# Two slot sums of a graph attention stream gathered in one PSUM bank before they are added

## The chip, the cores and the metric

The kernel runs on one core of one Trainium2 chip. The metric is the device time of one execution in microseconds (us). A NeuronCore has a matrix engine (TensorE, PE in the profile), a vector engine (VectorE, DVE), a scalar engine (ScalarE, ACT), GpSimd (POOL) and SyncE (SP); matmuls write to PSUM, a memory of eight banks of 512 fp32 words a partition, and DVE and ACT read it.

## The reference

Four graph attention layers run over one graph of 3125 nodes and 53125 edges (25000 pairs in both directions and 3125 loops; layers 0, 1 and 3 add another loop for each node, 56250 edges). Each layer is `x = x + layer(relu(layernorm(x)))` on 256 features. What the edge streams compute is this, here of layer 3, which has two such convolutions (4 heads of 64 channels and 8 heads of 32):

```python
h = (x @ W).reshape(n_nodes, heads, out_ch)
e = leaky_relu(alpha_s[src] + alpha_d[dst], 0.2)
m = segment_max(e, dst)
ex = exp(e - m[dst])
denom = segment_sum(ex, dst)
a = ex / (denom[dst] + 1e-16)
out = segment_sum(h[src] * a[:, :, None], dst)
```

Layers 0 and 1 have one convolution of 4 and of 8 heads over the same edges. Layer 2 has 4 heads, no added loops, edge weights, and sums over the source node instead of the destination.

## The kernel before

A first part sorts the edges twice, by destination (`by_dst`) and by source (`by_src`). A sorted edge list is cut in slots of 128 edges. All edges of a slot belong to one tile of 128 nodes (25 tiles; the last slot of a tile is filled up), so `by_dst` has 464 slots and `by_src` 448. `next_places` finds from a histogram how many slots each tile has, where they start, and which tile a slot belongs to; the tiles of four slots are packed into one integer of `tiles4` (lines 435 to 439). The layers follow one after the other. In each, `gat_layer` makes a table `feats` in DRAM with a row for each node (features, a one for each head, scores), and then `stream_edges` goes once over all slots.

In `stream_edges` the engines work so:

- GpSimd gathers the 128 rows of a slot from `feats` by an indirect DMA (line 1173), four slots a group, into a ring `rows` of 96 slots (48 in layer 3, which has NC = 2 convolutions and so rows twice as wide). A ring place is used again when `slot_sums` says that PE is through with it.
- For a chunk of CS slots (32 in layers 0 and 2, 16 in layers 1 and 3) a chain of four steps makes the probabilities: `score`, `largest`, `carries`, `shift` on DVE, each followed by a small PE piece (`turn_scores`, `turn_ends`, `turn_carry`, `turn_back`). The steps for chunk c+1 stand between the groups of chunk c. Where they stand says the tuple AT: in layers 1 and 3 `score` stands ahead of the chunk's first group of four slots, the others behind groups 0, 1 and 2. PE's `pick_own` fetches the node's own scores with one small matmul a slot (line 1235), in layers 1 and 3 eight of them behind groups 1 and 2.
- The gathered rows are multiplied by the probabilities: in layer 3 ACT does the first convolution slot by slot (line 1330, `messages_too`), DVE the second for four slots in one instruction (`scale`, line 1477, `messages`). With one convolution, DVE takes slots 0 and 2 of four, ACT slots 1 and 3.
- DVE makes a one-hot matrix `oh` of the destinations (`rows_onehot`, line 1459), in halves of two slots.
- PE multiplies one-hot by rows, one slot at a time, into a PSUM buffer of BANKS = 4 // NC, so four in layers 0 to 2 and two in layer 3 (`sums`, line 1281): 260 or 272 columns, or twice 264 in layer 3. Before it, PE waits until DVE has added the slot BANKS earlier (`added`).
- DVE adds the buffer to the accumulator `acc` of the slot's tile (`add`, line 1487), one instruction a slot; in layer 3 it reads both convolutions' banks at once, 528 columns. The tile number comes from `four_tiles` (line 80): a register load and arithmetic on the engine's sequencer.

Every engine's order is written out by hand and unrolled. On DVE a group of four slots is, in this order:

```python
ids = four_tiles(dve, g, gg, T)
if i == 0 and c > 0:
    rescale(c, ids[0])
add(gg, 0, ids)
scale(gg + 1)
add(gg, 1, ids)
rows_onehot(gg + 2, 0, 2)
add(gg, 2, ids)
rows_onehot(gg + 2, 2, 4)
add(gg, 3, ids)
chain(c + 1, i)
```

`rescale` (line 1451) multiplies the open tile's accumulator at a chunk's start by the factor by which the running maximum changed.

## Time and profile before

| | us |
|---|---|
| median of 3 runs | 4905.24 (4902.48 to 4909.39) |
| the profiled execution, its own time | 4901.73 |
| its span, first to last instruction | 4899.9 |
| busy in the span: PE, DVE, ACT, POOL | 3153.6, 3423.1, 2251.0, 2881.1 |
| edge stream of layer 0 (1526 to 2149) | 623 |
| edge stream of layer 1 (2290 to 2909) | 619 |
| edge stream of layer 2 (3049 to 3661) | 612 |
| edge stream of layer 3 (3870 to 4797) | 927 |

The busy times are sums over stages with different limits, so they name no single bound; what a stage waits for is read inside its window. The chain that ended last covers only the last few microseconds here and was not used.
### The profile page before, as it was taken

To read this page: it belongs to the slowest core of one execution; us is meant where nothing else is said; L and a number is where in the kernel's file an instruction comes from. 1 tells how busy PE (TensorE), PEld (TensorE's weight loads), DVE (VectorE), ACT (ScalarE), POOL (GpSimd) and SP (SyncE) were. 2 spreads that over 40 slices of the span, in tenths; PEclk is the share of its full clock that TensorE was granted. 3 is DMA by queue.
4 is the path that set the end of the run, shared out by engine and by line. 5 is a ranking of instruction groups with operands and counts; after the bars stand their busy time and mean duration, and the time that the engine had idled before them with its cause. 6 is when DMAs were issued, how large, how long until landed. Compare 5 with 4: busy or idle time off the path is not lost. (4 is left out here: it accounts for less than half of the span.)

```text
span 4899.9 us, 71994 instructions
## 1 busy us (share of the span) xinstructions
PE 3153.6 (64%) x13174; PEld 2163.4 (44%) x13174; DVE 3423.1 (70%) x11000; ACT 2251.0 (46%) x8908; POOL 2881.1 (59%) x2739
## 2 busy tenths in 40 slices
PE   1688885888534666646777754566654577777776
PEld 0466664666422444424444433344432344444444
DVE  5887775666454666675888883666763688888887
ACT  0355554555332333344666754233325354455545
POOL 0377776777607777715777734777730655555632
PEclk9955556555566777766777766777876788888989
DMA  1000000000024444414555523444431765555631
GB/s 50 1 2 2 2 2 2 2 2 2 3 65 143 133 123 131 126 20 131 146 144 142 147 56 117 121 131 132 131 45 54 224 169 163 163 164 162 169 83 61
DMA packets 235827, 448.84 MB, mean 92 GB/s; under 512 B 80264, under 2 KB 132390, under 8 KB 235110
## 3 DMA queue, kind: packets, MB, share of 16 engines
q0 software_dynamic: 130816, 317.16, 25.2%
q1 hardware_dynamic: 104752, 128.89, 8.1%
q8 instruction: 82, 1.34, 0.1%
q14 instruction: 177, 1.45, 0.1%
HBM read 416.04 MB, written 29.80 MB: 91 GB/s over the span
## 5 line engine op out<-in xcount | busy, mean ns | idle before, releaser
L1173 POOL DMA_INDIRECT rows.4<-feats,by_dst_other.1 x464 | 548.8, 1183 | 563.8 <-issue 343.1
L1173 POOL DMA_INDIRECT rows.1<-feats,by_dst_other.1 x464 | 490.1, 1056 | 280.1 <-POOLq L935 138.9
L1173 POOL DMA_INDIRECT rows.2<-feats,by_dst_other.1 x464 | 482.0, 1039 | 284.7 <-POOLq L935 143.5
L1173 POOL DMA_INDIRECT rows.3<-feats,by_src_other.1 x448 | 476.4, 1063 | 260.8 <-issue 131.1
L617 POOL DMA_INDIRECT by_dst_records<-r_rec.1,r_idx.1 x448 | 443.4, 990 | 156.3 <-issue 127.4
L617 POOL DMA_INDIRECT by_src_records<-r_rec.2,r_idx.2 x416 | 413.8, 995 | 143.6 <-issue 113.7
L1330 ACT ACTIVATE rows.4<-rows.4,xres.1 128x65 f32<-128x65 f32 x1856 | 448.0, 336 | 0.9
L1330 ACT ACTIVATE rows.2<-rows.2,e_prob.2 128x33 f32<-128x33 f32 x1856 | 397.9, 314 | 0.0
L1281 PE MATMUL m_p0.4<-rows.4,xres.1 128*128 128x264 f32 x928 | 311.0, 465 | 109.4 <-DVE acc.4 L1487 105.6
L1281 PE MATMUL m_p1.4<-rows.4,xres.1 128*128 128x264 f32 x928 | 318.2, 475 | 62.7 <-ACT rows.4 L1330 33.8
L1281 PEld LDWEIGHTS m_p1.4<-rows.4,xres.1 128*128 128x128 f32 x928 | 200.2, 230 | 159.1 <-ACT rows.4 L1330 81.1
L1281 PEld LDWEIGHTS m_p0.4<-rows.4,xres.1 128*128 128x128 f32 x928 | 189.8, 223 | 162.8 <-ACT rows.4 L1330 93.9
L561 PEld LDWEIGHTS r_pl.1<-k_table.1,r_loT.1 128*128 128x128 f32 x896 | 213.1, 327 | 40.5 <-issue 29.0
L1330 ACT ACTIVATE rows.1<-rows.1,e_prob.1 128x65 f32<-128x65 f32 x928 | 224.1, 335 | 0.5
L1487 DVE TENSOR_TENSOR acc.4<-acc.4,m_p0.4 128x528 f32 x232 | 163.4, 704 | 80.2 <-PE m_p0.4 L1281 39.5
L1330 ACT ACTIVATE rows.3<-rows.3,e_prob.3 128x65 f32<-128x65 f32 x896 | 216.3, 335 | 0.5
L561 PEld LDWEIGHTS r_pl.2<-k_table.2,r_loT.2 128*128 128x128 f32 x832 | 194.3, 322 | 37.4 <-issue 27.4
L1487 DVE TENSOR_TENSOR acc.4<-acc.4,m_p1.4 128x528 f32 x232 | 162.7, 701 | 53.4 <-PE m_p1.4 L1281 46.7
L1313 ACT ACTIVATE e_factor.4<-e_pc.4 128x12 f32<-128x12 f32 x29 | 5.3, 181 | 410.4 <-DVE xres.1 L1432 410.4
L561 PE MATMUL r_pl.1<-k_table.1,r_loT.1 128*128 128x25 f32 x896 | 190.9, 365 | 0.0
L1313 ACT ACTIVATE e_factor.1<-e_pc.1 128x4 f32<-128x4 f32 x15 | 2.6, 174 | 408.8 <-DVE e_chosen.1 L1432 408.8
L1313 ACT ACTIVATE e_factor.3<-e_pc.3 128x4 f32<-128x4 f32 x14 | 2.4, 174 | 402.4 <-DVE e_chosen.3 L1432 402.4
(764 smaller groups left out, 9190.7 us busy)
## 6 DMA issues: line engine op xcount, KB each, us to landing
e_line.1<-by_dst_own_row SPq DMA_DIRECT2D x29, 512.0 KB, 4.9
e_line.2<-by_dst_own_row SPq DMA_DIRECT2D x29, 512.0 KB, 4.6
e_line.4<-by_dst_own_row SPq DMA_DIRECT2D x58, 256.0 KB, 5.2
e_line.3<-by_src_own_row SPq DMA_DIRECT2D x28, 512.0 KB, 5.0
xres.1<-by_dst_masks SPq DMA_DIRECT2D x232, 48.0 KB
e_mask.2<-by_dst_masks SPq DMA_DIRECT2D x29, 320.0 KB
rows.1<-feats,by_dst_other.1 POOLq DMA_INDIRECT x464, 2.9
rows.2<-feats,by_dst_other.1 POOLq DMA_INDIRECT x464, 4.0
```

The source lines that it names most:

```text
L561: ins = pe.matmul(p_look[:, j, 0:T], ohloT[:, j, :], g.k_table[:, quarter % 2, j, :], start=True, stop=True)
L617: pool.indirect_dma_start(out=g.records, out_offset=bass.IndirectOffsetOnAxis(ap=idx[:, quarter, j:j + 1], axis=0), in_=rec[:, quarter, j, ...
L1173: pool.indirect_dma_start(out=rows[:, s % RING, :], out_offset=None, in_=feats, in_offset=bass.IndirectOffsetOnAxis(ap=g.other[:, s:s + 1] ...
L1281: ins = pe.matmul(pp[s % BANKS][:, k, 0:AW], oh[:, gg % 3, j, :], rows[:, s % RING, row0[k]:row0[k] + AW], start=True, stop=True)
L1313: act.activation(factor[:, :], pcar[:, FACT:FACT + HS], ACT.Exp).then_inc(S["rescale"].sem, 1)
L1330: ins = act.activation(part, part, ACT.Copy, scale=prob[:, c % 2, i, heads0[k] + h:heads0[k] + h + 1])
L1487: dve.tensor_tensor(a, a, pp[s % BANKS][:, :, 0:AW], ALU.add).then_inc(S["added"].sem, 1)
```

## The change

For the two uses of `by_dst` (layers 0, 1 and 3; `paired` is true where loops are added) the sums of two slots of one node tile are gathered in one PSUM bank by accumulating matmuls, and DVE adds once for the two. A chunk of m slots has m/2 + 1 groups. Each even slot opens a group, and the last slot opens one of its own. An odd slot joins either the group of the slot after it or that of the slot before it: the one ahead if both are of one tile, else the one behind. Which it is, PE reads from a new table `joined4` and puts into the bank's address by a register. Every tile gets at least two slots, so one of the two always fits. A group is closed by a matmul of one zero column for each convolution, which signals `closed`; DVE waits for this and adds to the tile of the group's base, read from a new table `bases4`. In layer 3 the addition is two instructions of 264 columns, one for each convolution, and PE may open the next group's first convolution after the first of them. `next_places` makes the two tables. The number of groups does not depend on the data: 247 in layer 0, 261 in layers 1 and 3.

```diff
@@ Graph
+        self.paired = loops
@@ new functions
+def base_tiles(eng, g, word, T, first, last):
+    v = eng.value_load(g.bases4[0:1, bass.ds(word, 1)], min_val=0, max_val=T ** 4 - 1)
+    before = None if first else eng.snap(v % T)
+    here = eng.snap((v // T) % T)
+    return (before, here, eng.snap((v // T ** 2) % T), eng.snap(v // T ** 3)) if last else (before, here)
+
+def joined_ahead(eng, g, word, first):
+    v = eng.value_load(g.joined4[0:1, bass.ds(word, 1)], min_val=0, max_val=15)
+    middle = (eng.snap(v % 2), eng.snap((v // 4) % 2))
+    return (None if first else (eng.snap((v // 2) % 2), eng.snap(v // 8)), middle)
@@ next_places, DVE
+            if g.paired:
+                link(dve.tensor_scalar(nslot[:, 0:T - 1], nslot[:, 0:T - 1], 2.0, None, ALU.max))
...
+            if g.paired:
+                W4 = SLOTS // 4
+                link(dve.scalar_tensor_tensor(tp[:, :], four[:, :, 3], float(T), four[:, :, 2], ALU.mult, ALU.add))
+                link(dve.scalar_tensor_tensor(tp[:, :], tp[:, :], float(T), four[:, :, 0], ALU.mult, ALU.add))
+                link(dve.tensor_scalar(tp[:, :], tp[:, :], float(T), None, ALU.mult))
+                link(dve.tensor_tensor(tp[:, 1:W4], tp[:, 1:W4], four[:, 0:W4 - 1, 2], ALU.add))
+                link(dve.tensor_copy(g.bases4[:, :], tp[:, :]))
+                link(dve.memset(alike[:, :], 0.0))
+                link(dve.tensor_tensor(alike[:, 4:SLOTS + 3], tf[:, 0:SLOTS - 1], tf[:, 1:SLOTS], ALU.is_equal))
+                link(dve.tensor_scalar(apart[:, :], alike[:, :], -1.0, 1.0, ALU.mult, ALU.add))
...
+                link(dve.scalar_tensor_tensor(tp[:, :], no_before, 2.0, no, ALU.mult, ALU.add))
+                link(dve.scalar_tensor_tensor(tp[:, :], tp[:, :], 2.0, yes_before, ALU.mult, ALU.add))
+                link(dve.scalar_tensor_tensor(g.joined4[:, :], tp[:, :], 2.0, yes, ALU.mult, ALU.add))
@@ stream_edges
+    def group0(c):
+        return c * (CS // 2 + 1)
+    def released(gg):
+        return max(summed_by(s) for s in range(4 * gg, 4 * gg + 4))
+    def group_added(k):
+        return (k + 1 + k // (CS // 2 + 1)) * NC
...
-        pp = [ps(f"m_p{j}", [P, NC, 512], F32, c2) for j in range(BANKS)]
+        pp = ps("m_p", [P, BANKS, NC, 512], F32, c2)
@@ stream_edges, PE
+            def opening(s, group):
+                scaled(s)
+                for k in range(NC):
+                    if group >= BANKS:
+                        pe.wait_ge(S["added"].sem, S["added"].at(group_added(group - BANKS) - NC + 1 + k))
+                    ins = pe.matmul(pp[:, group % BANKS, k, 0:AW], oh[:, s // 4 % 3, s % 4, :],
+                                    rows[:, s % RING, row0[k]:row0[k] + AW], start=True, stop=False)
+                ins.then_inc(S["slot_sums"].sem, 1)
+
+            def joining(s, group, ahead):
+                scaled(s)
+                to, back = group % BANKS, (group - 1) % BANKS
+                at = pe.snap(ahead[0] + back) if to > back else pe.snap(ahead[1] * back)
+                for k in range(NC):
+                    ins = pe.matmul(pp[:, bass.ds(at, 1), k, 0:AW].rearrange("p a f -> p (a f)"), oh[:, s // 4 % 3, s % 4, :],
+                                    rows[:, s % RING, row0[k]:row0[k] + AW], start=False, stop=False)
+                ins.then_inc(S["slot_sums"].sem, 1)
+
+            def closing(group):
+                for k in range(NC):
+                    pe.matmul(pp[:, group % BANKS, k, 0:1], zeros[:, :], zeros[:, 0:1], start=False, stop=True).then_inc(S["closed"].sem, 1)
...
-                    sums(gg, 0)
-                    sums(gg, 1)
+                    group = group0(c) + 2 * i
+                    if PAIRS:
+                        before, middle = joined_ahead(pe, g, gg, i == 0)
+                        opening(s0 + 4 * i, group)
+                        if i > 0:
+                            joining(s0 + 4 * i - 1, group, before)
+                            closing(group - 1)
...
-                    sums(gg, 2)
-                    sums(gg, 3)
+                    if PAIRS:
+                        opening(s0 + 4 * i + 2, group + 1)
+                        joining(s0 + 4 * i + 1, group + 1, middle)
+                        closing(group)
+                        if i == m // 4 - 1:
+                            closing(group + 1)
+                            opening(s0 + m - 1, group + 2)
+                            closing(group + 2)
@@ stream_edges, DVE
+            def add_group(c, k, tile):
+                group = group0(c) + k
+                dve.wait_ge(S["closed"].sem, S["closed"].at(NC * (group + 1)))
+                if group:
+                    dve.wait_ge(S["added"].sem, S["added"].at(group_added(group - 1) + (NC if k == 0 else 0)))
+                for k in range(NC):
+                    a = acc[:, bass.ds(tile, 1), k * AW:(k + 1) * AW].rearrange("p a f -> p (a f)")
+                    dve.tensor_tensor(a, a, pp[:, group % BANKS, k, 0:AW], ALU.add).then_inc(S["added"].sem, 1)
...
+                        tiles = base_tiles(dve, g, gg, T, i == 0, last)
+                        if i == 0 and c > 0:
+                            rescale(c, tiles[1])
+                        if i > 0:
+                            add_group(c, 2 * i - 1, tiles[0])
+                        scale(gg + 1)
+                        rows_onehot(gg + 2, 0, 2)
+                        add_group(c, 2 * i, tiles[1])
+                        rows_onehot(gg + 2, 2, 4)
+                        if last:
+                            add_group(c, 2 * i + 1, tiles[2])
+                            add_group(c, 2 * i + 2, tiles[3])
```

`scaled(s)` holds the waits for `messages` and `messages_too` that `sums` had. `zeros` is a 128x128 bf16 tile, set once a layer.

## Rows read from the trace of the kernel before

**Rows 1.** Windows of three edge streams: us, busy time of each engine, PEclk, DMA share, GB/s
```profile
1526.00:2149.00 623.00, 392.35 (x1470) 267.35 (x1469) 425.39 (x1142) 231.43 (x957) 445.91 (x422) 0.74 0.43 118
2290.00:2909.00 619.00, 462.18 (x1607) 282.54 (x1605) 518.27 (x1475) 411.81 (x1926) 446.23 (x430) 0.72 0.49 133
...
3870.00:4797.00 927.00, 688.12 (x2558) 455.69 (x2558) 765.11 (x1559) 467.95 (x1916) 511.10 (x429) 0.87 0.56 154
```
**Rows 2.** Groups by line of the page: count | busy us, mean ns | idle us before, releaser
```profile
L1173 POOL DMA_INDIRECT rows.1<-feats,by_dst_other.1 x464 | 490.1, 1056 | 280.1 <-POOLq L935 138.9 <-issue 135.1 <-PE m_p0.1 L1281 4.0
L1173 POOL DMA_INDIRECT rows.2<-feats,by_dst_other.1 x464 | 482.0, 1039 | 284.7 <-POOLq L935 143.5 <-issue 131.4 <-PE m_p2.2 L1281 9.4
```
**Rows 3.** Waits of the whole execution: us in total, times, longest us
```profile
DVE e_scores.1 L1389 <- DMA rows.1<-feats,by_dst_other.1: 137.6, 14, 20.5
```
**Rows 4.** Line 1173, GpSimd's idle time before a gather: us, times
```profile
  PE m_p2.2 L1281: 9.4, 31
```
**Rows 5.** Groups by line, the additions of layers 3 and 1
```profile
L1487 DVE TENSOR_TENSOR acc.4<-acc.4,m_p0.4 128x528 f32 x232 | 163.4, 704 | 80.2 <-PE m_p0.4 L1281 39.5 <-issue 29.6 <-PE m_p1.4 L1281 7.8
L1487 DVE TENSOR_TENSOR acc.4<-acc.4,m_p1.4 128x528 f32 x232 | 162.7, 701 | 53.4 <-PE m_p1.4 L1281 46.7 <-issue 0.3
...
L1487 DVE TENSOR_TENSOR acc.2<-acc.2,m_p3.2 128x272 f32 x116 | 50.8, 438 | 4.1 <-issue 1.0 <-PE m_p1.2 L1281 0.6 <-DVE acc.2 L1487 0.3
```
**Rows 6.** Timeline of layer 3, DVE in an iteration: start us, us, what
```profile
4755.24 1.25 DVE L1477 TENSOR_TENSOR rows.4<-rows.4,xres.1 128x1056 f32<-128x1056 f32 x1
...
4756.40 0.70 DVE L1487 TENSOR_TENSOR acc.4<-acc.4,m_p1.4 128x528 f32 x1
4757.02 0.42 DVE L1459 TENSOR_TENSOR xres.1<-iota_row.1,by_dst_klo.1 128x256 f32<-128x256 f32 x1
...
4759.21 0.17 DVE L1416 COPY e_end.4<-e_pc.4 12x32 f32<-12x32 f32 x1
...
4761.76 0.70 DVE L1487 TENSOR_TENSOR acc.4<-acc.4,m_p0.4 128x528 f32 x1 [0.57 <-issue]
```
**Rows 7.** Timeline of layer 3's last slots, PE and DVE
```profile
4792.80 1.13 PE L1281 MATMUL m_p0.4<-rows.4,xres.1 128*128 128x264 f32 x4
4793.14 0.70 DVE L1487 TENSOR_TENSOR acc.4<-acc.4,m_p1.4 128x528 f32 x1 [0.49 <-PE m_p1.4 L1281]
...
4793.99 1.13 PE L1281 MATMUL m_p1.4<-rows.4,xres.1 128*128 128x264 f32 x4
4794.19 0.70 DVE L1487 TENSOR_TENSOR acc.4<-acc.4,m_p0.4 128x528 f32 x1 [0.34 <-PE m_p0.4 L1281]
```
**Rows 8.** Timeline of layer 3, PE around eight selection matmuls (4734.60 to 4736.36)
```profile
4730.22 1.97 PE L1281 MATMUL m_p1.4<-rows.4,xres.1 128*128 128x264 f32 x4
...
4732.71 1.16 PE L1281 MATMUL m_p0.4<-rows.4,xres.1 128*128 128x264 f32 x4
...
4733.71 1.05 PE L1281 MATMUL m_p1.4<-rows.4,xres.1 128*128 128x264 f32 x4
...
4736.36 1.13 PE L1281 MATMUL m_p0.4<-rows.4,xres.1 128*128 128x264 f32 x4
```
**Rows 9.** Line 1384, once a chunk in layer 3, between 4320 and 4780 us
```profile
L1384 DVE TENSOR_REDUCE xres.1<-e_po.4 x14: 750/751/751, 4320.2 to 4743.4; 128x192 f32<-128x576 f32 x14
```
**Rows 10.** Timeline of layer 3, DVE from the scores to the next addition
```profile
4743.39 0.75 DVE L1384 TENSOR_REDUCE xres.1<-e_po.4 128x192 f32<-128x576 f32 x1
...
4746.35 0.70 DVE L1487 TENSOR_TENSOR acc.4<-acc.4,m_p0.4 128x528 f32 x1
```
**Rows 11.** Lines 80 and 1235, PE's sequencer: count: ns min/median/max, first and last start
```profile
L80 PEldq TENSOR_LOAD <-by_dst_tiles4.1 x348: 295/301/491, 1480.3 to 4734.8; - x174
...
L1235 PEldq FUSED_REGOPS  x1840: 91/122/151, 1481.1 to 4736.1; - x184
```
**Rows 12.** Timeline of the setup, DVE in `next_places` on one partition
```profile
173.98 0.63 DVE L435 TENSOR_SCALAR h_tf.1<-h_pt.1 1x464 f32<-1x464 f32 x1 [1.86 <-PE h_pt.1 L406]
...
175.41 0.35 DVE L439 SCALAR_TENSOR_TENSOR by_dst_tiles4.1<-h_tp.1,h_tf.1 1x116 int32<-1x116 f32 x1
```

More of the change, by code:

```diff
@@ L404, in _ @@
             pe.matmul(px[:, 1, 0:T], ones[:, :], counts[:, :], start=True, stop=True).then_inc(totals.sem, 1)
-            pe.wait_ge(cnt.sem, cnt.at(13))
+            pe.wait_ge(cnt.sem, cnt.at(14 if g.paired else 13))
             pe.matmul(pt[:, 0:SLOTS], ones[0:T, 0:1], ge[:, :], start=True, stop=True).then_inc(totals.sem, 1)
@@ L1082, in stream_edges @@
     BANKS = 4 // NC
+    PAIRS = g.paired
     AT = (3, 4, 5, 6) if CS == 32 else (-1, 0, 1, 2)
@@ L1101, in added_by, with summed_by @@
         return s + 1 + chunk_of(s) * NC
+    def group0(c):
+        return c * (CS // 2 + 1)
+    def summed_by(s):
+        c = chunk_of(s)
+        s0, m = chunks[c]
+        i = s - s0
+        if not PAIRS or i in (0, m - 1):
+            return s + 1
+        return s + 2 if i % 2 else s
+    def released(gg):
+        return max(summed_by(s) for s in range(4 * gg, 4 * gg + 4))
+    def group_added(k):
+        return (k + 1 + k // (CS // 2 + 1)) * NC
     def halves(c):
@@ L1133, in stream_edges @@
         chosen = room("e_chosen", [P, 2, FOLDS, FS])
+        zeros = sb("m_zeros", [P, P], BF16, c2) if PAIRS else None
         line = sb("e_line", [P, 2, HALF * P], BF16, c2)
@@ L1168, in _ @@
                 if nb >= RB:
-                    pool.wait_ge(S["slot_sums"].sem, S["slot_sums"].at(4 * (nb - RB + 1)))
+                    pool.wait_ge(S["slot_sums"].sem, S["slot_sums"].at(released(nb - RB)))
                     pool.sem_inc(S["row_gate"].sem, 1)
@@ L1294, in _ @@
                     gg = s0 // 4 + i
-                    sums(gg, 0)
-                    sums(gg, 1)
+                    group = group0(c) + 2 * i
[5 more added lines that the diff above has]
+                            closing(group - 1)
+                    else:
+                        sums(gg, 0)
+                        sums(gg, 1)
                     if c + 1 < NCH:
@@ L1300, in _ @@
                                 turn(c + 1)
-                    sums(gg, 2)
-                    sums(gg, 3)
+                    if PAIRS:
[6 more added lines that the diff above has]
+                            closing(group + 2)
+                    else:
+                        sums(gg, 2)
+                        sums(gg, 3)
                     if CS == 32:
@@ L1348, in link @@
                 dve.wait_ge(S["chain"].sem, S["chain"].at(steps[0]))
+            if PAIRS:
+                dve.memset(zeros[:, :], 0.0)
             link(dve.memset(end[:, :, :], 0.0))
@@ L1446, in rescale @@
                 dve.wait_ge(S["rescale"].sem, S["rescale"].at(c + 1))
-                dve.wait_ge(S["added"].sem, S["added"].at(added_by(chunks[c][0] - 1)))
+                dve.wait_ge(S["added"].sem, S["added"].at(group_added(group0(c) - 1) if PAIRS else added_by(chunks[c][0] - 1)))
                 for k, cv in enumerate(convs):
@@ L1516, in _ @@
                     gg = s0 // 4 + i
-                    ids = four_tiles(dve, g, gg, T)
-                    if i == 0 and c > 0:
-                        rescale(c, ids[0])
-                    add(gg, 0, ids)
-                    scale(gg + 1)
-                    add(gg, 1, ids)
-                    rows_onehot(gg + 2, 0, 2)
-                    add(gg, 2, ids)
-                    rows_onehot(gg + 2, 2, 4)
-                    add(gg, 3, ids)
+                    if PAIRS:
+                        last = i == m // 4 - 1
+                        tiles = base_tiles(dve, g, gg, T, i == 0, last)
[10 more added lines that the diff above has]
+                            add_group(c, 2 * i + 2, tiles[3])
+                    else:
+                        ids = four_tiles(dve, g, gg, T)
+                        if i == 0 and c > 0:
+                            rescale(c, ids[0])
+                        add(gg, 0, ids)
+                        scale(gg + 1)
+                        add(gg, 1, ids)
+                        rows_onehot(gg + 2, 0, 2)
+                        add(gg, 2, ids)
+                        rows_onehot(gg + 2, 2, 4)
+                        add(gg, 3, ids)
                     chain(c + 1, i)
@@ L1530, in stream_edges @@
                       messages_too=SLOTS if NC == 2 else NG * len(BY_ACT), slot_sums=SLOTS,
-                      added=SLOTS + (NCH - 1) * NC, row_gate=NG - RB)
+                      closed=(SLOTS // 2 + NCH) * NC if PAIRS else 0,
+                      added=(SLOTS // 2 + NCH) * NC + (NCH - 1) * NC if PAIRS else SLOTS + (NCH - 1) * NC, row_gate=NG - RB)
         for name in ("own_summed", "scored", "turned", "topped", "ends_out", "carried", "carry_out", "carry_read", "rescale", "shifted", "exps",
```

22 lines of the change are left out of this document (18 added, 4 removed).

## The prediction

> **What bounds the kernel now.** I read the stretches of the four edge streams first. Three of the streams run the changed code: layers 0, 1 and 3. Layer 2 sorts by source, is not paired, and stays as it is. The windows of layers 0 and 1 are 623 and 619 us long, that of layer 3 is 927 us [rows 1]. VectorE (DVE) is busy 425, 518 and 765 us in them, so each saved addition looks attractive. The next view asks what each stream waits for.
>
> In layer 0 GpSimd issues 464 gathers, 490.1 us busy with 135.1 us of gaps between issues: 625 us, the whole stream [rows 2]. DVE waits 137.6 us for those gathers, in 14 waits, one a chunk [rows 3]. An addition saved there lengthens this wait. In layer 1 the same two numbers are 482.0 and 131.4, together 613 us against a window of 619; GpSimd waited for a freed row buffer for only 9.4 us [rows 1, 2, 4]. So layer 1 can gain at most these 9 us and something after its last gather.
>
> Layer 3 is the stream where DVE is the pace. A chunk of 16 slots takes (4743.4 - 4320.2) / 13 = 32.55 us [rows 9]. Its additions read two banks at once, 704 ns each, against 438 ns for the one-bank addition of layer 1 [rows 5]. So the question is what a chunk of layer 3 becomes.
>
> **DVE's work in a chunk of layer 3.** Starts of successive instructions give the real pitch: scaling 1.17 us (4755.24 to 4756.40), addition 0.62 us, half a one-hot, 0.42 us long, 0.41 [rows 6]. A small chain step follows each four slots: 2.55 us from 4759.21 to the next addition at 4761.76 [rows 6]; its sisters of the iterations before and after, read the same way, are 2.78 and 2.88 us, and scores with rescaling 2.96 us (4743.39 to 4746.35) [rows 10]. Sum: 16 x 0.62 + 4 x 1.17 + 8 x 0.41 + 11.2 = 29.1 us, so 3.4 us of waiting are in the 32.55.
>
> After the change there are 9 groups a chunk with two additions of 264 columns. Their pitch I take as 0.34 us, the one-bank 0.43 us less the overlap of about 0.09 which the 704 ns addition shows against its pitch of 0.62 [rows 5, 6]. 18 x 0.34 = 6.1 us in place of 9.9: DVE saves 3.8 us a chunk, and its own sum is 25.3 us. If nothing else moved, layer 3 would lose 28 x 3.8 = 106 us.
>
> **What the pairs do to the two banks.** Layer 3 has BANKS = 2. Today slot s waits for the addition of slot s-2, while slot s-1 is being multiplied, so PE and DVE overlap. After the change PE's order is: open group g, join a slot, close g-1, open g+1. Opening g+1 needs the bank of g-1, closed one instruction earlier. Nothing of the row sums lies between the closing and this wait, so PE stands still for the whole turn-around. The end of the stream prices it: PE's slot ends at 4793.93 and its addition starts at 4794.19; an addition ends at 4793.84 and the next slot starts at 4793.99 [rows 7]. With the first addition of 0.43 us that is 0.22 + 0.43 + 0.15 = 0.8 us of PE time per group. (I use 0.22, as the modelled matmul ends give 0.20 to 0.26.) The pair itself is two slots back to back, 1.00 + 1.05 us [rows 8]. The two closing matmuls are not in the trace; below, they can't cost less than nothing, above, I bound them by eight selection matmuls with their register work, 1.6 us, or 0.2 us each [rows 8]. I take 0.2 us for both. A turn of one group is then 0.8 + 2.05 + 0.2 = 3.05 us, and DVE cannot start the next addition earlier.
>
> Put around the chunk, at the upper clock: the half of an iteration with scaling has 2.26 us of DVE work (0.68 + 1.17 + 0.41) against 3.05 us, three times, with about 0.6 us more for the small transposes between: 9.8 us. The half with the chain step after iteration 0 is 0.68 + 0.41 + 2.78 = 3.9 us, DVE's. In iterations 1 and 2 eight selection matmuls follow the closing, 1.6 us, and then the new word of registers: a load of 0.30 and two register steps of 0.12 to 0.15 us [rows 11]; 2.2 + 2.05 + 0.2 + 0.22 = about 4.6 us each, against 3.6 to 4.0 of DVE. Chunk end and the start of the next are DVE's: three groups with a wait for the lone last slot (3.0), scores and rescaling (3.6 with register issue), scaling and one-hot (1.6): 8.2 us. Total 9.8 + 3.9 + 9.2 + 8.2 = 31.1 us.
>
> That is at the upper clock. The stream's mean granted clock is 0.87, so about a quarter of the time lies at 1.2 GHz [rows 1]; a slot takes 1.97 us there and not 1.05 [rows 8]. DVE hides most of that now. After the change about 11 of 16 slots are on the path, some 0.25 of them slow, 0.92 us each: 2.6 us. New chunk 33.7 us, 1.15 more than 32.55; 28 chunks give **+32 us**. The last chunk has no chain steps to cover the turns: its 16 slots take 19.2 us now, and about 24 with six turns of 3.05, its two ends and one slow stretch: **+5 us**.
>
> A rule speaks here too. The Trainium skill (TensorE: Matmul & The Clock Gate, "A second HAM failure mode: psum-queue depth-cycling") says that an engine which idles briefly between matmul groups as it cycles through banks swings between the two clocks and loses throughput. The trace shows such swinging already (0.72 to 0.87); whether the new 0.8 us gaps add to it no row shows. Should they, the lower-clock rival below has its price.
>
> **The other terms.** Setup: twelve more linked DVE instructions on the serial path, eight of 116 elements at 0.35 us and the gap of 0.03 that linked instructions leave, three of about 464 at 0.63 and the same gap, one tiny: **+5 us** [rows 12]. Layer 0: its gathers cover everything; after the last of them the rest of one chunk and the last chunk remain, 8 iterations that lose 0.7 us of additions each and gain one lone group or two: **-5 us**. Layer 1: up to 9.4 us of waits and 8 such iterations behind its last gather [rows 4], but PE gets 116 register words (0.57 us each, 66 us), 261 closings (0.1 to 0.2, some 40) and 232 register steps (28 us) beside its 462 busy of 619 us [rows 1, 11]: it comes to about 596, close to full. I take **-4 us**, between -15 and +20. The memset of zeros and the reshaped PSUM tensor cost nothing; row buffers come free about one slot later, which the ring of 48 covers.
>
> Sum: 32 + 5 + 5 - 5 - 4 = **+33 us**. The profiled execution took 4901.7 us (span 4899.9), 3.5 us below the median of 4905.2; so 4935 for it, **4938 us** for the median.
>
> **The rivals.** (1) *DVE stays the pace in layer 3.* The clock stays high since PE is asked for more densely, closings are nearly free, and the selection matmuls are prefetched during the pair: a chunk of 29.4 to 31.1 us. At 30.5, 28 x 2.05 = 57 us less, with the last chunk and the other terms about -56: 4849 us. For it: DVE's chain steps are 11.2 of 32.55 us. Against: the turn of 3.05 us exceeds 2.26 in three halves. It decides where a new chunk falls below 32.2 us. Chance 0.26. (2) *The gain and the turn-around cancel*: chunk at 32.2 to 32.8, about 4905. Chance 0.13. (3) *PE becomes the pace in layers 0 and 1 too*, by register words and closings; four banks hide the turn but not the load. +5% on both is 60 us on top: 4998. For it: 596 of 619. Against: layer 0 has 10 us of slack a chunk. Chance 0.12. (4) *The clock falls in layer 3* to the 0.72 of layer 1 [rows 1]: twice the slow share, 3 to 4 us more a chunk, about 5035. Chance 0.09. My forecast, +11 to +75 us, has 0.40. That pairs fail to join is no case: there is one group per two slots whatever the tiles are.
>
> **Range and chances.** 4850 to 5020 leaves the stronger half of (1) and the far part of (3) and (4) outside; the forecast's own range is 4915 to 4980. 0.2% (10 us) is about what a measurement can tell from no change. Faster 0.26, same 0.13, slower 0.61.
>
> **What would show it.** In the profile after: in layer 3, the additions of 264 columns at 0.43 us, x261 twice; DVE busy about 100 us less; DVE's idle time before additions, now 80.2 + 53.4 us [rows 5], grown to over 200 us and released by the closing; PE idle before openings, released by the addition, some 0.6 us a time; chunk about 33.7 us. Layers 0 and 1 within 10 us of now. The forecast is wrong if PE's closings cost over 0.4 us (slower), if the granted clock in layer 3 moves by more than 0.05 (either way), or if GpSimd stops being the pace in layer 1.

## The result, and the profile after

The changed kernel takes **4871.76 us** (median of 4 runs, 4867.77 to 4873.72) against 4903.86 us (4901.02 to 4909.39) for the kernel before on the same chip: ratio 0.9934, 95% interval 0.992 to 0.9948. It is 32 us faster; the forecast was 33 us slower. The profiled execution took 4869.96 us, with a span of 4868.2 us.

The first view is again that of the three changed streams, engine by engine, with the columns of [rows 1]:

```profile
1531.00:2149.00 618.00, 403.16 (x1716) 278.52 (x1714) 345.00 (x922) 230.76 (x955) 446.10 (x422) 0.73 0.43 119
2292.00:2916.00 624.00, 481.42 (x1865) 319.30 (x1863) 439.34 (x1269) 409.25 (x1915) 457.13 (x429) 0.70 0.49 132
3878.00:4764.00 886.00, 635.70 (x3075) 476.92 (x3074) 647.86 (x1615) 464.18 (x1900) 471.00 (x426) 0.91 0.57 160
```

DVE's busy time fell by 80, 79 and 117 us, but only layer 3 became much shorter. From the first gather of a stream to the start of its last addition, the distances are (before, after): layer 0 678.7 and 674.6, layer 1 664.3 and 671.4, layer 2 668.1 and 665.9, layer 3 973.7 and 936.5. With 4.5 us more of setup, that is -4.1 + 7.1 - 2.2 - 37.2 + 4.5 = -31.9 us; the spans differ by 31.7.

The groups by line that answer to [rows 2, 5]: the gather of layer 1, the openings of layer 3, the additions, and the closings of layer 3 (line 1381):

```profile
L1237 POOL DMA_INDIRECT rows.2<-feats,by_dst_other.1 x464 | 494.5, 1066 | 279.6 <-POOLq L976 138.5 <-issue 135.0 <-PE m_p.2 L1364 5.8
L1364 PE MATMUL m_p.4<-rows.4,xres.1 128*128 128x264 f32 x1044 | 324.0, 438 | 145.7 <-DVE acc.4 L1613 109.8 <-issue 24.8 <-ACT rows.4 L1445 9.3
L1613 DVE TENSOR_TENSOR acc.4<-acc.4,m_p.4 128x264 f32 x522 | 200.4, 425 | 219.3 <-PE m_p.4 L1381 183.6 <-issue 28.9 <-DVE acc.4 L1613 6.6
L1613 DVE TENSOR_TENSOR acc.2<-acc.2,m_p.2 128x272 f32 x261 | 113.7, 436 | 145.0 <-PE m_p.2 L1381 105.0 <-issue 31.6 <-DVE acc.2 L1613 8.0
L1381 PE MATMUL m_p.4<-m_zeros.3 128*128 128x1 bf16 x522 | 47.5, 168 | 0.0
```

In layer 3 DVE now idles 219 us ahead of additions, 183.6 of them released by a closing, and PE idles 109.8 us ahead of openings, released by an addition. Most of this is the turn-around of the two banks, as the prediction had it (the halves with selections, below, are in it too). The same turn in the timeline of layer 3 (start us, us, what):

```profile
4300.19 0.77 DVE L1613 TENSOR_TENSOR acc.4<-acc.4,m_p.4 128x264 f32 x2 [0.49 <-issue]
...
4300.77 1.13 PE L1364 MATMUL m_p.4<-rows.4,xres.1 128*128 128x264 f32 x4 [0.18 <-DVE acc.4 L1613]
...
4301.73 1.05 PE L1374 MATMUL m_p.4<-rows.4,xres.1 128*128 128x264 f32 x4
...
4302.63 0.24 PE L1381 MATMUL m_p.4<-m_zeros.3 128*128 128x1 bf16 x4
4303.13 0.77 DVE L1613 TENSOR_TENSOR acc.4<-acc.4,m_p.4 128x264 f32 x2 [0.48 <-PE m_p.4 L1381]
4303.71 1.13 PE L1364 MATMUL m_p.4<-rows.4,xres.1 128*128 128x264 f32 x4 [0.84 <-DVE acc.4 L1613]
```

From addition to addition it is 2.94 us, PE idles 0.84 us of it; the prediction had 3.05 and 0.8. Yet the chunk is shorter. This is the score instruction of each chunk, on DVE, after (line 1501); that of before, over the same 28 scores, is the second row:

```profile
L1501 DVE TENSOR_REDUCE xres.1<-e_po.4 x28: 748/750/751, 3869.4 to 4712.8; 128x192 f32<-128x576 f32 x28
```

```profile
L1384 DVE TENSOR_REDUCE xres.1<-e_po.4 x28: 750/751/751, 3865.1 to 4743.4; 128x192 f32<-128x576 f32 x28
```

(4743.4 - 3865.1) / 27 = 32.53 us before, and (4712.8 - 3869.4) / 27 = **31.24 us** after, where 33.7 was forecast. 27 x 1.29 = 35 us is nearly all that layer 3 gained.

Where in the chunk? I took the starts of all additions of these chunks from the timeline and averaged the distances. 0 to 8 are the nine groups. "Shortest" is the shortest of the 27 values of that distance, each column by itself, and its sum is the sum of these: no chunk has them all, and the shortest whole chunk took 30.11 us.

```
us from              score-0  0-1   1-2   2-3   3-4   4-5   5-6   6-7   7-8  8-score  sum
after, mean            4.73   3.86  2.97  5.67  3.72  4.24  3.14  1.10  1.12  0.69   31.24
after, shortest        4.54   3.80  2.93  4.39  2.93  3.89  2.93  1.09  1.05  0.68   28.23
```

The halves 1-2, 3-4 and 5-6 are the turns behind a scaling; 2-3 and 4-5 hold the chain step and eight selection matmuls. Half 2-3 is far from its shortest in nearly every chunk (over 5 us in 26 of 27). The granted clock explains it. Here the stretches of one such half and of the one after it (us, busy PE, PEld, DVE, ACT, POOL, granted clock, DMA share, GB/s):

```profile
4315.00:4317.00 2.00, 2.00 (x13) 1.64 (x13) 1.63 (x3) 1.43 (x6) 1.73 (x1) 1.00 0.53 137
4317.00:4319.50 2.50, 1.13 (x9) 0.61 (x8) 2.03 (x9) 0.00 (x0) 1.89 (x3) 1.00 0.54 130
4319.50:4320.50 1.00, 1.00 (x4) 0.88 (x5) 0.69 (x3) 0.00 (x0) 0.33 (x1) 0.83 0.65 214
4320.50:4327.00 6.50, 6.50 (x19) 4.80 (x18) 2.28 (x4) 0.00 (x0) 3.03 (x3) 0.50 0.37 100
4327.00:4330.00 3.00, 2.33 (x20) 1.84 (x19) 2.31 (x8) 0.18 (x1) 1.04 (x2) 1.00 0.72 194
```

And PE in the same stretch:

```profile
4316.85 0.52 PE L1299 MATMUL e_po.4<-e_parts.4,e_hot.4 128*128 x4
...
4318.01 0.79 PE L1299 MATMUL e_po.4<-e_parts.4,e_hot.4 128*128 x4 [0.65 <-issue]
...
4319.42 1.38 PE L1364 MATMUL m_p.4<-rows.4,xres.1 128*128 128x264 f32 x4 [0.62 <-issue]
...
4320.59 1.97 PE L1374 MATMUL m_p.4<-rows.4,xres.1 128*128 128x264 f32 x4
...
4322.86 0.77 DVE L1613 TENSOR_TENSOR acc.4<-acc.4,m_p.4 128x264 f32 x2 [2.56 <-PE m_p.4 L1381]
```

PE does eight tiny selections in 2.5 us, with two gaps in which its sequencer reads words of registers (one for the next four selections, one for the joinings). It was busy for 1.13 of 2.5 us, then the grant fell to 1.2 GHz and stayed there for some 6.5 us. DVE waited 2.56 us for the pair. In 25 of the 27 chunks the grant fell inside half 2-3, each time to 1.2 GHz and for 3.4 or 6.8 us.

The last chunk but one has no selections (nor gathers) beside it. From its score at 4712.8 us to its last addition at 4739.7 the changed kernel took 26.96 us, half 2-3 took 3.58, and the clock did not fall; before, the same chunk took 31.62 us.

```profile
4712.80:4740.00 27.20, 17.95 (x93) 14.00 (x93) 21.93 (x56) 16.27 (x68) 0.00 (x0) 1.00 0.00 1
```

### The profile page after: what moved, and what is told of

Its sections match the earlier page's. It is cut to its first block and busy times, and to the rows that moved or that the text cites. A ratio compares the mean times of both kernels' runs of the same rounds, so it can differ in the third digit from the quotient of the medians.

```text
span 4868.2 us, 74715 instructions
## 1 busy us (share of the span) xinstructions
PE 3104.0 (64%) x14124; PEld 2235.3 (46%) x14204; DVE 3152.1 (65%) x10653; ACT 2250.4 (46%) x8908; POOL 2855.3 (59%) x2739
## 5 line engine op out<-in xcount | busy, mean ns | idle before, releaser
L1237 POOL DMA_INDIRECT rows.4<-feats,by_dst_other.1 x464 | 511.5, 1102 | 564.8 <-issue 342.1
L1237 POOL DMA_INDIRECT rows.2<-feats,by_dst_other.1 x464 | 494.5, 1066 | 279.6 <-POOLq L976 138.5
L1364 PE MATMUL m_p.4<-rows.4,xres.1 128*128 128x264 f32 x1044 | 324.0, 438 | 145.7 <-DVE acc.4 L1613 109.8
L1613 DVE TENSOR_TENSOR acc.4<-acc.4,m_p.4 128x264 f32 x522 | 200.4, 425 | 219.3 <-PE m_p.4 L1381 183.6
L1345 PE MATMUL m_p.3<-rows.3,m_oh.3 128*128 128x260 f32 x896 | 309.2, 497 | 16.4 <-DVE rows.3 L1594 15.5
L1364 PE MATMUL m_p.2<-rows.2,m_oh.2 128*128 128x272 f32 x522 | 259.5, 600 | 29.9 <-issue 17.2
L1364 PEld LDWEIGHTS m_p.4<-rows.4,xres.1 128*128 128x128 f32 x1044 | 192.1, 205 | 184.8 <-issue 122.3
L1374 PE MATMUL m_p.4<-rows.4,xres.1 128*128 128x264 f32 x812 | 253.9, 442 | 0.0
L1364 PE MATMUL m_p.1<-rows.1,m_oh.1 128*128 128x260 f32 x494 | 219.6, 542 | 40.3 <-issue 19.4
L1345 PEld LDWEIGHTS m_p.3<-rows.3,m_oh.3 128*128 128x128 f32 x896 | 205.7, 247 | 77.3 <-DVE rows.3 L1594 32.6
L1604 DVE TENSOR_TENSOR acc.3<-acc.3,m_p.3 128x260 f32 x448 | 189.3, 423 | 62.5 <-PE m_p.3 L1345 29.3
L602 PEld LDWEIGHTS r_pl.2<-k_table.2,r_loT.2 128*128 128x128 f32 x832 | 194.3, 321 | 37.5 <-issue 27.5
L1613 DVE TENSOR_TENSOR acc.2<-acc.2,m_p.2 128x272 f32 x261 | 113.7, 436 | 145.0 <-PE m_p.2 L1381 105.0
```

Source lines behind the costliest of these rows:

```text
L602: ins = pe.matmul(p_look[:, j, 0:T], ohloT[:, j, :], g.k_table[:, quarter % 2, j, :], start=True, stop=True)
L1237: pool.indirect_dma_start(out=rows[:, s % RING, :], out_offset=None, in_=feats, in_offset=bass.IndirectOffsetOnAxis(ap=g.other[:, s:s + 1] ...
L1345: ins = pe.matmul(pp[:, s % BANKS, k, 0:AW], oh[:, gg % 3, j, :], rows[:, s % RING, row0[k]:row0[k] + AW], start=True, stop=True)
L1364: ins = pe.matmul(pp[:, group % BANKS, k, 0:AW], oh[:, s // 4 % 3, s % 4, :], rows[:, s % RING, row0[k]:row0[k] + AW], start=True, stop=False)
L1374: ins = pe.matmul(pp[:, bass.ds(at, 1), k, 0:AW].rearrange("p a f -> p (a f)"), oh[:, s // 4 % 3, s % 4, :], rows[:, s % RING, row0[k]:row ...
L1604: dve.tensor_tensor(a, a, pp[:, s % BANKS, :, 0:AW], ALU.add).then_inc(S["added"].sem, 1)
```

## The experiments

Besides the first (the pairs taken back out of layers 0 and 1) each kernel changes layer 3 alone, and all but the last have pairs in layer 3 alone or in none. "Chunk" is the distance of the scores in layer 3 over 27 chunks, read as above; "layer 3" goes from first gather to last addition; "clock" is the mean granted clock of that stream, without its first 50 us or so, which in every one of these kernels lie at 1.2 GHz. Chunk, layer 3 and clock come from the one profiled execution of each kernel, so differences of a few us in them are not told apart from scatter. Ratios are to the kernel before, on the same chip as each.

| | what | us | ratio, 95% | chunk | layer 3 | clock |
|---|---|---|---|---|---|---|
| before | | 4903.86 | 1 | 32.53 | 973.7 | 0.87 |
| after | | 4871.76 | 0.9934 (0.992-0.9948) | 31.24 | 936.5 | 0.91 |
| e1 | pairs in layer 3 alone | 4876.03 | 0.9941 (0.9929-0.9954) | 31.08 | 931.5 | 0.91 |
| e2 | one addition of 528 columns | 4886.68 | 0.9964 (0.9951-0.9976) | 31.54 | 945.9 | 0.91 |
| e3 | split closings | 4819.05 | 0.9824 (0.9812-0.9837) | 29.16 | 875.9 | 0.95 |
| e4 | zero matmuls, no pairs | 4904.07 | 0.9997 (0.9987-1.0008) | 32.25 | 964.2 | 0.88 |
| e5 | words read ahead | 4863.15 | 0.9928 (0.9907-0.9948) | 30.96 | 928.2 | 0.92 |
| e6 | e3 and e5 | 4810.56 | 0.9824 (0.9799-0.9849) | 29.11 | 874.5 | 0.94 |
| e7 | no words for selections | 4778.44 | 0.9757 (0.9737-0.9776) | 27.86 | 844.6 | 1.00 |
| e8 | no words for joinings | 4778.06 | 0.9757 (0.9738-0.9777) | 27.80 | 843.0 | 1.00 |
| e9 | selections spread | 4780.64 | 0.9747 (0.9732-0.9762) | 27.87 | 845.0 | 0.99 |
| e10 | e3 and e9 | 4753.72 | 0.9692 (0.9677-0.9707) | 26.95 | 816.3 | 0.99 |
| e11 | selections spread, no pairs | 4877.34 | 0.994 (0.9923-0.9957) | 31.47 | 943.9 | 0.90 |
| e12 | e10, pairs in layers 0, 1, 3 | 4756.93 | 0.9701 (0.968-0.9722) | 27.07 | 819.4 | 0.98 |

**e1, pairs in layer 3 alone.**

```diff
-    PAIRS = g.paired
+    PAIRS = g.paired and n == 3
```

> Pairs in layer 3 alone; layers 0 and 1 run the sums of the kernel before (the tables are still made). Theory A, each stream's difference belongs to its own edit: layer 3 is 37 us shorter, the setup 4.5 us longer, layers 0 and 1 as before, so 4903.9 - 37.2 + 4.5 - 2 = about 4869, within 3 us of the changed kernel; first gather to last addition of layer 1 is back at 664 us. Rival B, the 7 us of layer 1 are scatter between executions: layer 1 stays anywhere between 664 and 672. Rival C, what layer 3 gained is scatter or clock: layer 3 lies off 936 us by more than 10.

Ratio 0.9941 against 0.9934: layer 3 carries the whole gain, and it is no scatter (4876 us against the 4869 of theory A, but 931.5 us in layer 3 against 936.5). Layer 1 without pairs took 669.2 us here, which leaves A and B open for its 7 us (see e12).

**e2, one addition for both convolutions.**

```diff
-                for k in range(NC):
-                    a = acc[:, bass.ds(tile, 1), k * AW:(k + 1) * AW].rearrange("p a f -> p (a f)")
-                    dve.tensor_tensor(a, a, pp[:, group % BANKS, k, 0:AW], ALU.add).then_inc(S["added"].sem, 1)
+                a = acc[:, bass.ds(tile, 1), :].rearrange("p a (k f) -> p (a k) f", k=NC)
+                dve.tensor_tensor(a, a, pp[:, group % BANKS, :, 0:AW], ALU.add).then_inc(S["added"].sem, NC)
```

> As the first run of this call, but the pair takes one addition of 528 columns after both closings. Theory A, the turn-around of the two banks sets three to five of the eight halves of a chunk: the first bank comes free after 0.70 and not 0.43 us, so 5 x 0.27 = 1.4 us a chunk more, against 9 x 0.06 us that one instruction is shorter than two: +0.8 to +1.4 us a chunk, layer 3 +25 to +40 us. Rival B, DVE's own work is the pace: -9 x 0.06 us a chunk, layer 3 -5 to -15 us.

The sign is A's, the size about half of it: layer 3 is 14.4 us longer than in e1, the chunk 0.46 us, the median of all runs 10.7 us. The turn rose from 2.94 to 3.20 us (medians of 1-2, 3-4 and 5-6), about the 0.27 us by which the first bank comes free later. Besides these three halves only 7-8 shows it (0.19 us longer); 0-1 is 0.08 us shorter, as DVE's own work is. So the second instruction of the pair is worth some 11 to 14 us.

**e3, split closings.** Convolution 0 of a joining is closed before convolution 1 is multiplied.

```diff
 def joining(s, group, ahead, done):
...
     for k in range(NC):
         ins = pe.matmul(pp[:, bass.ds(at, 1), k, 0:AW]..., start=False, stop=False)
+        if k == NC - 1:
+            ins.then_inc(S["slot_sums"].sem, 1)
+        closing(done, k)
-    ins.then_inc(S["slot_sums"].sem, 1)
...
 def add_group(c, k, tile):
-    dve.wait_ge(S["closed"].sem, S["closed"].at(NC * (group + 1)))
+    dve.wait_ge(S["closed"].sem, S["closed"].at(NC * group + 1))
...
     for k in range(NC):
+        if k:
+            dve.wait_ge(S["closed"].sem, S["closed"].at(NC * group + k + 1))
```

> As the first run, but a joining multiplies convolution 0, closes it, then multiplies convolution 1 and closes it, and each addition waits for its own closing. The first addition then runs under the second convolution's multiplication. Theory A, the turn-around is on the path: 0.5 to 0.6 us less in each half that it sets, 3 to 5 of them a chunk, so 2 us a chunk and layer 3 shorter by 40 to 60 us. Rival B, DVE's own work sets the chunk: layer 3 within 5 us of the first run.

Theory A holds: layer 3 is 55.6 us shorter than in e1, the chunk 1.92 us. The turns fell to 2.43, 2.62 and 2.45 us (medians). In its timeline DVE adds convolution 0 while PE multiplies convolution 1, and the next opening no longer waits for an addition:

```profile
4300.41 0.61 PE L1374 MATMUL m_p.4<-rows.4,xres.1 128*128 128x264 f32 x2
4300.86 0.17 PE L1383 MATMUL m_p.4<-m_zeros.1 128*128 128x1 bf16 x1
4300.89 0.69 PE L1374 MATMUL m_p.4<-rows.4,xres.1 128*128 128x264 f32 x2
...
4301.32 0.87 DVE L1615 TENSOR_TENSOR acc.4<-acc.4,m_p.4 128x264 f32 x2
4301.41 0.22 PE L1383 MATMUL m_p.4<-m_zeros.1 128*128 128x1 bf16 x3
4301.89 1.13 PE L1364 MATMUL m_p.4<-rows.4,xres.1 128*128 128x264 f32 x4 [0.26 <-ACT rows.4 L1445]
```

The turn was on the path, then, and the changed kernel gained in spite of it. Part of the 1.92 us is the clock, 0.95 in place of 0.91: the means of the three turns fell by 1.26 us together, half 2-3 by 0.94 with its shortest unchanged (4.38 for 4.39), and half 4-5 rose by 0.24.

**e4, zero matmuls without pairs.**

```diff
-    PAIRS = g.paired
+    PAIRS = False
+    EXTRA = n == 3
...
-                                    rows[:, s % RING, row0[k]:row0[k] + AW], start=True, stop=True)
+                                    rows[:, s % RING, row0[k]:row0[k] + AW], start=True, stop=not (EXTRA and j % 2))
+                if EXTRA and j % 2:
+                    for k in range(NC):
+                        ins = pe.matmul(pp[:, s % BANKS, k, 0:1], zeros[:, :], zeros[:, 0:1], start=False, stop=True)
                 ins.then_inc(S["slot_sums"].sem, 1)
```

> No pairs at all, but in layer 3 each second slot of the kernel before is ended by the two matmuls of one zero column for its two convolutions. Theory A, the closing matmuls cost about 0.1 us each on PE and change no clock: layer 3 is 0 to 15 us longer than before (974 us) with a granted clock of 0.86 to 0.88; the setup adds 4.5 us, so 4908 to 4923. Rival B, the small matmuls themselves raised the clock in the changed kernel: granted clock 0.90 or more and layer 3 not longer than before.

The clock stayed at 0.88, so the zero matmuls do not raise it. No cost of theirs shows either: layer 3 is 9.5 us shorter than before, where A had 0 to 15 longer, and the total is the same (0.9997), where A had 4908 to 4923 us. Why it is shorter was not followed up; the two are one execution each.

**e5, words read ahead, and e6, the same with split closings.**

```diff
                     elif c + 2 < NCH and i in (1, 2):
-                        pick_own(c + 2, 8, 8 * (i - 1))
...
+                        w0 = chunks[c + 2][0] // 4 + 2 * (i - 1)
+                        words = [four_tiles(pe, g, w0, T), four_tiles(pe, g, w0 + 1, T)]
+                        loaded = joined_ahead(pe, g, gg + 1, False)
+                        pick_own(c + 2, 8, 8 * (i - 1), words)
```

> Pairs in layer 3 alone, and there PE reads the two words with the tiles of the next eight selections and the word for the next joinings before the selections, while it multiplies the pair, not between them. Theory A, the gaps of 0.65 and 0.62 us around the selections are this register work, and the granted clock falls behind them: the half behind group 1 goes from 5.6 to 4.4 us, the two after it lose their slow part (0.8 and 0.3 us), the chunk 31.1 to 29.0 us, layer 3 shorter by 45 to 60 us and its granted clock 0.94 or more. Rival B, the clock falls for another reason: the two gaps go (1.2 us in one half of a chunk at most), the clock stays at 0.91, layer 3 shorter by 10 to 30 us. Rival C, the register work only moves and delays the next opening: no change.

> The earlier words of e5 together with the split closings of e3. Theory A, with the turn covered the selections' gaps are hidden in part already (granted clock 0.95 in e3): another 5 to 20 us below e3, about 4805. Rival B, DVE is the pace already after e3: within 5 us of e3, 4815 to 4822.

A fell for this edit, and B; it is C, with 3.3 us in layer 3. The gap did not vanish, it moved ahead of the selections, and the selections themselves came at longer distances:

```profile
4322.18 0.19 PE L1381 MATMUL m_p.4<-m_zeros.1 128*128 128x1 bf16 x2
...
4323.31 1.65 PE L1299 MATMUL e_po.4<-e_parts.4,e_hot.4 128*128 x8 [0.94 <-issue]
...
4324.90 1.68 PE L1364 MATMUL m_p.4<-rows.4,xres.1 128*128 128x264 f32 x4
...
4326.37 1.97 PE L1374 MATMUL m_p.4<-rows.4,xres.1 128*128 128x264 f32 x4
```

The stretch from 4322.4 to 4324.9 is again 2.5 us long, the clock falls behind it as before (0.92 in the mean), and e6 equals e3, as its rival B had it. Three words in a row, moved ahead of the selections, left the same gap and the same lower clock.

**e7, no words for the selections, and e8, none for the joinings.** e7 selects fixed tiles behind groups 1 and 2 of a chunk, so that the scores are those of other nodes; e8 sends each odd slot to the group after it, so that some sums land in the wrong tile, and reads no word of `joined4` anywhere in the stream.

```diff
-                        pick_own(c + 2, 8, 8 * (i - 1))
+                        pick_own(c + 2, 8, 8 * (i - 1), [(0, 1, 2, 3), (4, 5, 6, 7)] if PAIRS else None)
```

```diff
-                at = pe.snap(ahead[0] + back) if to > back else pe.snap(ahead[1] * back)
                 for k in range(NC):
-                    ins = pe.matmul(pp[:, bass.ds(at, 1), k, 0:AW].rearrange("p a f -> p (a f)"), oh[...],
+                    ins = pe.matmul(pp[:, to, k, 0:AW], oh[...],
...
-                        before, middle = joined_ahead(pe, g, gg, i == 0)
+                        before = middle = None
```

> Pairs in layer 3 alone; behind groups 1 and 2 the selections there take fixed tiles, so PE loads no words for them (the scores computed are those of other nodes). Theory A, as for e5, a little more since the word for the joinings alone is left: layer 3 shorter by 45 to 65 us, clock 0.94 or more. Rival B, the clock falls for another reason: shorter by 10 to 25 us at 0.91.

> Pairs in layer 3 alone; each odd slot of layer 3 joins the group after it at a fixed address, so PE reads no words for the joinings (the sums then land in the wrong tile where two slots lie apart). Theory A, the word matters only where PE's sequencer is not ahead, behind the selections: 0.6 us in two halves of a chunk at most, layer 3 shorter by 10 to 35 us. Rival B, the word is hidden everywhere by the wait for the bank: within 5 us of e1.

Either edit alone takes 87 to 89 us out of layer 3, more than either theory gave, and the granted clock, once up, does not fall again before the stream ends. Half 2-3 of e8 is 3.57 to 3.64 us in every chunk (5.59 in the mean in e1), 3-4 is 2.94 again. The same stretch of e8, and its stream:

```profile
4326.96 0.25 PE L1299 MATMUL e_po.4<-e_parts.4,e_hot.4 128*128 x4
...
4327.82 0.79 PE L1299 MATMUL e_po.4<-e_parts.4,e_hot.4 128*128 x4 [0.61 <-issue]
...
4328.56 1.13 PE L1364 MATMUL m_p.4<-rows.4,xres.1 128*128 128x264 f32 x4
```

```profile
3879.00:4670.00 791.00, 560.49 (x3074) 428.95 (x3074) 646.90 (x1612) 462.39 (x1893) 481.80 (x426) 1.00 0.63 179
```

The gap of 0.61 us is still there; the second one is not, and the opening follows 1.35 us after the end of the first four selections and not 2.05. So the register work costs twice: 0.8 us in half 2-3 directly (4.39 at the shortest in e1, 3.58 in the mean here), and the rest of the 3.28 us a chunk, about 2.5, by the lower clock that follows it.

**e9, selections spread.** As many words as in the changed kernel, all of them used, but four selections in each of four places.

```diff
+                    if n == 3 and c + 2 < NCH and i == 3:
+                        pick_own(c + 2, 4, 12)
                     if c + 1 < NCH:
                         for k, turn in enumerate(turns):
...
-                    elif c + 2 < NCH and i in (1, 2):
+                    elif n == 3 and c + 2 < NCH and i < 3:
+                        pick_own(c + 2, 4, 4 * i)
+                    elif n != 3 and c + 2 < NCH and i in (1, 2):
                         pick_own(c + 2, 8, 8 * (i - 1))
```

> Pairs in layer 3 alone; there PE makes four selections behind groups 0, 1 and 2 and four ahead of the second half of group 3, each with its own word, in place of eight behind groups 1 and 2. The words are as many as in the changed kernel, but none stands beside another word of selections. Theory A, the clock fell because PE had almost nothing to multiply for some 2 us while its sequencer read three words in a row: granted clock 0.98 or more, the half behind group 1 at 3.6 to 4.2 us, a chunk from score to score 27.8 to 28.6 us against 31.1 in e1, layer 3 shorter than in e1 by 65 to 90 us, total near 4790 to 4815. Rival B, it is the number of words that counts: clock 0.92, within 20 us of e1.

Theory A: chunk 27.87 us, half 2-3 3.59 us, layer 3 86.5 us shorter than in e1, ratio 0.9747; the 4781 us lie 9 us below the total that A had. The stream:

```profile
3877.00:4677.00 800.00, 548.98 (x3086) 423.47 (x3086) 652.27 (x1620) 469.39 (x1922) 498.50 (x431) 0.99 0.64 180
```

PE still idles at the chunk's start, and no fall follows:

```profile
4323.99 0.42 PE L1308 MATMUL e_pt.4<-ident.1,xres.1 128*96 128x128 f32 x2 [1.62 <-DVE xres.1 L1511]
4324.26 1.06 PE L1364 MATMUL m_p.4<-rows.4,xres.1 128*128 128x264 f32 x4
```

**e10, spread and split.** Both diffs.

> e9 with the split closings of e3. Theory A, both gains hold where they act, the turn (0.5 us in three halves of a chunk) and the clock: layer 3 shorter than in e9 by 30 to 45 us, total 4750 to 4780. Rival B, DVE's own 25.3 us and the chunk end are then the pace, and half of it is left: 4775 to 4800.

Ratio 0.9692, 150 us below the kernel before, where the change had 0.9934. Layer 3 is 28.7 us shorter than in e9: the three turns gave 0.51 us each, but 2-3, 4-5 and 6-7 took back 0.35, 0.13 and 0.12. The two additions of groups 2, 4 and 6 now start 0.46 us apart in place of 0.35; what else is in the 0.35 was not broken down. That is a little under A's 30 to 45, and not B's half.

**e11, spread without pairs in any layer.**

> No pairs in any layer, the spread selections of e9 in layer 3. Theory A, the kernel before lost some 1.9 us a chunk to the lower clock (its halves at their shortest sum to 30.7 us, not 32.5): layer 3 shorter by 30 to 55 us than before, total 4860 to 4880 with the setup's 5 us, and pairs are then worth 50 to 70 us at one clock (e9 against this run). Rival B, unpaired, PE's sums already cover the selections: within 15 us of before.

30 us less in layer 3, as A had it at its low end, and 4877 in all. But the clock is 0.90, not 1.00, and what lowers it there was not looked into. Against this run the pairs are worth 943.9 - 845.0 = 99 us in layer 3, where I had expected 50 to 70; with the selections in eights they are worth 973.7 - 931.5 = 42.

**e12, e10 with pairs in layers 0 and 1 too.**

> As e10, with pairs in layers 0 and 1 too, as in the changed kernel. First gather to last addition: layer 0 674 to 676 us (674.6 in the changed kernel, 677.5 to 678.8 unpaired in five runs). Theory A, layer 1's 671.4 us in the changed kernel was PE's register words and lower clock (0.70): 669 to 673 us again, against 664 to 669 unpaired. Rival B, it was scatter: 664 to 668 us. Either way the total stays within 8 us of e10, ratio to before 0.967 to 0.972.

Layer 1 took 672.8 us. Paired, it is 671.4 and 672.8; unpaired, in twelve profiled executions (before and e1 to e11), 664.3 to 670.2 with a mean of 667. So A's number came, about 5 us lost, at a clock of 0.69 and 0.70 against 0.71 to 0.73 unpaired. A's cause, PE, did not show. The gathers of layer 1 say where the time is. These are before, after, e10 (unpaired in this layer) and e12: ns of one (shortest, median, longest), first and last start.

```profile
L1173 POOL DMA_INDIRECT rows.2<-feats,by_dst_other.1 x464: 1017/1022/1345, 2243.8 to 2866.0; - x155
L1237 POOL DMA_INDIRECT rows.2<-feats,by_dst_other.1 x464: 1013/1019/1507, 2243.9 to 2878.5; - x155
L1237 POOL DMA_INDIRECT rows.2<-feats,by_dst_other.1 x464: 1017/1022/1406, 2248.8 to 2875.3; - x155
L1237 POOL DMA_INDIRECT rows.2<-feats,by_dst_other.1 x464: 1015/1019/1508, 2246.0 to 2881.3; - x155
```

From first to last gather it is 622 to 629 us in the twelve unpaired executions and 634.6 and 635.4 in the paired ones. GpSimd's gaps between them add up to 141 us in all fourteen, so the whole difference is in the gathers' own time (482 to 489 us unpaired, 494.5 and 495.2 paired). Behind the last gather the pairs saved 5 us, as forecast (41.3 to 42.1 us unpaired, 36.8 and 37.4 paired). GpSimd is still the pace. Why its gathers take longer beside pairs is open; PE's register words or its clock may be behind it, but no run tried that. Layer 0 took 677.4 us and misses its forecast of 674 to 676; paired it is 674.6 and 677.4, unpaired 677.5 to 680.1. The two layers together are worth nothing that the total shows (0.9701 against 0.9692, intervals overlapping).

## Why the prediction was wrong

The sign hung on the chunk of layer 3, forecast at 33.7 us and measured at 31.24. The 4871.76 us lie inside the stated range of 4850 to 5020, but only because that range reached into rival 1, on the other side of no change; the forecast's own range, 4915 to 4980, missed. By the prediction's own steps:

- **Base.** 32.55 us a chunk; all 27 give 32.53. Right.
- **DVE's own work.** Additions of 264 columns at 0.425 us in the mean, x522; DVE busy 117 us less (about 100 forecast). Right.
- **The turn-around.** Right in mechanism and nearly in size: 2.94 us for 3.05, and 0.84 us of PE's idle time in the turn shown for 0.8. e3 shows that it was on the path, e2 that the first bank's release sets it.
- **The chunk at the upper clock, 31.1 us: this is the step that failed.** The halves at their shortest sum to 28.2. I was high in each: the three turns 9.8 for 8.8, because I added 0.6 us for transposes that run inside the turn and because of the 0.1 on each turn; the halves with selections 4.6 + 4.6 for 4.39 + 3.89, because PE's sequencer runs ahead during the pair, so that the first four (or all eight) selections start the moment the closings end; the chunk end and the next start 8.2 for 7.36, of which 0.7 in the scores, rescaling, scaling and one-hot (3.6 + 1.6 for 4.54). Together 9.8 + 3.9 + 9.2 + 8.2 = 31.1 against 8.8 + 3.8 + 8.3 + 7.4 = 28.2. Whole chunks at the upper clock bear it out: the last but one, without selections, took 26.96 us to its last addition, and the shortest of e7, e8 and e9, which save 0.8 us, took 27.5.
- **The lower clock, +2.6 us.** Mean less shortest is 31.24 - 28.23 = 3.0 us: right in size. Only the place was unknown to me: it is not spread over a quarter of the slots, it sits behind the selections of group 1, once a chunk in nearly all, and e7, e8 and e9 remove it.
- **Last chunk, +5 us.** Right in sign: between the last addition of the chunk before it and its own last addition it is 20.3 us before and 23.0 after, +2.7. The chunk ahead of it, counted among the 28 at +1.15, came out 4.7 us shorter (31.6 to 27.0); it has no selections, and its clock did not fall.
- **Setup +5:** 4.5. **Layer 0 -5:** -4.1 here, and some 2.5 by all fourteen executions. **Layer 1 -4, between -15 and +20:** +7.1, of which e12 and the unpaired runs leave about 5 as the pairs' own. The 5 us behind the last gather came, the 9.4 us of GpSimd's waits gave nothing (its gaps are 141 us as before), and the gathers themselves took some 10 us more, a term that the prediction did not have. Layer 2, unchanged, came out 2.2 us shorter.

In sum: 33 forecast, less 27 x 2.46 = 66 for the chunks, less 6 for the last but one, less 2 for the last, plus 11 for layer 1, plus 1 for layer 0, less 2 for layer 2: -31, against -31.9 in the profiled executions. One term of 2.9 us a chunk turned the sign.

Rival 1 (DVE keeps the pace, closings nearly free, selections prefetched, chunk 29.4 to 31.1) comes nearest, with the chunk just above its upper end. Its conditions: no cost of the closings seen (e4), selections prefetched in part (the trace), clock 0.91 and not 0.87. Its first words, that DVE stays the pace, are wrong for the turns: e3 shows PE and DVE waiting for each other there. Rival 3 (PE becomes the pace in layers 0 and 1) did not come: layer 1 lost 5 us, against 60 for the two, and GpSimd stayed the pace. Rival 4, a falling clock, did not come.

On the banks: before its openings of layer 3, PE idled 109.8 us for an addition in the changed kernel and 110.8 us in e8, with the same turns of 2.94 us, and in e7, e8 and e9 the granted clock was 1.00 over 788 us. The line and the stream of e8:

```profile
L1364 PE MATMUL m_p.4<-rows.4,xres.1 128*128 128x264 f32 x1044 | 295.1, 406 | 115.2 <-DVE acc.4 L1612 110.8 <-ACT rows.4 L1444 2.6 <-DVE rows.4 L1593 1.7
```

```profile
3883.00:4671.00 788.00, 556.70 (x3064) 426.07 (x3062) 645.20 (x1608) 458.45 (x1876) 478.72 (x423) 1.00 0.63 179
```

The rule of the Trainium skill that the prediction weighed (TensorE: Matmul & The Clock Gate, "A second HAM failure mode: psum-queue depth-cycling"), that short idling between groups in cycling through banks makes the clock swing, is not borne out for these gaps; the case that the Trainium skill tells of there is bf16 with 512 columns, this one is fp32 with 264. In the changed kernel's layer 3 the swing was there, but it came from register work beside eight tiny matmuls, not from the banks.

## What to carry to other kernels

Add up a changed loop at one clock, each term from the shortest rows, and only then add what the lower clock costs; terms set a little high one by one made 10% of a chunk here. When two engines hand two buffers back and forth, signal each part of the buffer as it is done: the split closings gave 57 us (e1 to e3), the whole change 32. Look where the matrix engine has only tiny matmuls and register reads to do, and spread them among the long ones.
